# Turning the softmax tile p of a cross-attention kernel: from TensorE transposes to a transposing DMA of two float16 parts

## Chip, cores and metric

The kernel runs on one core of a Trainium2 chip. The metric is the device time of one execution in microseconds (us); lower is better. Engines: PE is TensorE (matmuls; PEld its weight loads), DVE is VectorE, ACT is ScalarE, POOL is GpSimd, SP is the sync engine, whose only work here is to issue DMAs.

## What is computed

One layer of cross-attention and one feed-forward product, in float32, for x of 32 batches x 64 tokens x 512 and a context of the same shape. All 32 query heads have width 128; 8 key/value heads are shared by four query heads each.

```python
q = rope(layernorm(x) @ Wq)        # 32 heads x 128
k = rope(ctx @ Wk); v = ctx @ Wv   # 8 heads x 128
s = q @ k.T / sqrt(128); s = where(mask == 0, -1e9, s)
p = softmax(s)                     # 64 x 64 per batch and head
x = x + (p @ v) @ Wo
x = x + layernorm(x) @ dequant(mxfp4(kernel)) + bias
```

## The kernel before, in words

**Precision by splitting.** Every operand of the large products is held as a high part (rounded to TensorE's fast 32-bit format, fp32r) and a low part (the rest). A product is then three matmuls (high x high, high x low, low x high), in the helper `three` (L539 to L541) and in `project_o` (L725 to L727). For p @ v two matmuls do: the 128 partitions of VS hold the high part of v in one half and the low part in the other; PS holds the high part of p in both halves, PL the low part of p in one half and zeros in the other (L703, L704).

**Stages and pairs.** The work is cut into 128 pairs m (PAIRS): one key/value head with its four query heads, for two batches of 64 tokens. A software pipeline runs over stages n; each engine has its own hand-written order within a stage, and all waits are semaphores. With m = n - 5, PE's stage n (L783 to L821) is `project_q(n)` (12 matmuls), `scores(m)` (4 products in 8 passes into pS), `turn_p(m-1)`, `values(m-2)`, then in some stages the K projection, the V projection, the FFN product, and `project_o(n-8)` (12 matmuls). The stages from n = 128 on have no `project_q`; in stages 130 to 136 there follow the last eight layer-norm and FFN tiles (`turn_f`, `ffn_high`, `ffn_low`).

**The path of p.** DVE masks the scores and takes the row maximum (L1336, L1339); ACT takes exp with the sum of each row (L1002); DVE takes the reciprocal and writes the normalised p to the SBUF tile sm (`p_scaled`, L1137 to L1145). One stage later PE turns sm in two 128x128 transposes into the PSUM tile pT (`turn_p`, L676 to L688). ACT casts two halves of pT to PS (`p_high`, L915), DVE subtracts to make PL (L1357 to L1361), ACT copies both halves of PS to the other partitions (L1007 to L1010), and one stage later PE uses them in `values` (L690 to L705).

**Orders around the change.** ACT's stage n is: `exchange` of the q tile for rope (L923, L924), rope tables, `v_high`, `x_high`, `f_high`, the weight casts `high` (L830), `p_high(m-1)`, exp(m), the PS copies, `out_high(m-2)` (L907), and `f_split_high`; from stage 130 on `out_high` stands ahead of exp. DVE's stage n begins with the sum of the output projection (`acc`, L1282), which waits for the end of PE's `project_o` of the stage before; then come layer-norm statistics, the low part of v, `f_low` (L1103) and `normalise` (L1067) in the last stages, rope's cos product, mask and maximum of pair m, the PL subtraction, steps of the mxfp4 quantisation (stages 10 to 55, in the other half of pT), `p_scaled(m)`, `out_low(m-2)`, and `ffn_add` (L1114). From stage 130 on `out_low` stands ahead of `p_scaled`.

**SP's queue.** SP runs one list of DMA issues, each behind its own wait (L492 to L529). In a stage n: the weight loads due in it, a raw x tile, stores, mask rows, and for the eight FFN tiles of the middle (f = 0 to 7, stages 69 to 76) the transposing DMA `turn_split(f)` (L470 to L478), which turns a 128 x 1024 float16 tile and which `ffn_high` waits for. From stage 130 on the store of FFN tile n-122 is issued in SP's stage n (L499, L500); it waits (L462) for the `ffn_add` of that tile, which DVE does in its stage n+1.

Of the kernel before, what the change touches and what calls it, by code (L numbers as in the profile page):

```python
# [86 lines left out]
PART = [range(0, 1), range(1, 4), range(4, 8)] + [range(k, k + 1) for k in range(8, QUANT)]  # L87

def quant_steps(n):  # L90

    parts = quant_parts(n)
    return sum(QUANT * i + PART[c].stop for i, c in parts[-1:]) if parts and parts[-1][1] < len(PART) else (
        QUANT * parts[-1][0] + QUANT if parts else 0)
# [29 lines left out]
def streamed(n):  # L124
    return [i for i, w in enumerate(STREAM) if w[0] == n]
# [48 lines left out]
def build(nc, x, ctxT, pos, mask, wq, wk, wv, wo, fkT, fbias, table, eye, out):  # L174
    ctx = ExitStack()
    with ctx:
        def sb(name, shape, dt):
            return ctx.enter_context(nc.sbuf_tensor(name, shape, dt))
# [8 lines left out]
        with ExitStack() as loads:  # L187
# [11 lines left out]
        kT = sb("kT", [128, 2, 512], F32)  # L199
        VS, PS = sb("VS", [128, 2, 8, 256], F32R), sb("PS", [128, 2, 256], F32R)  # L200
        QH, KH = sb("QH", [128, 4, 4, 128], F32R), sb("KH", [128, 4, 128], F32R)
# [4 lines left out]
        t2, t3 = sb("t2", [128, 512], F32), sb("t3", [128, 512], F32)  # L206
        PL = sb("PL", [128, 2, 256], F32R)
        sm = sb("sm", [128, 256], F32)
        ident = sb("ident", [128, 128], F32)
# [31 lines left out]

        d_ft = sem("d_ft")
# [3 lines left out]
        e_qk, e_pt, e_pv, e_op = sem("e_qk"), sem("e_pt"), sem("e_pv"), sem("e_op")  # L246
        e_ft, e_fm, e_wt = sem("e_ft"), sem("e_fm"), sem("e_wt")
# [3 lines left out]
        a_hi, a_xh, a_cs, a_ex = sem("a_hi"), sem("a_xh"), sem("a_cs"), sem("a_ex")  # L251
        a_ph, a_px, a_ah, a_vh, a_fh, a_w4 = (sem("a_ph"), sem("a_px"), sem("a_ah"), sem("a_vh"), sem("a_fh"),
                                              sem("a_w4"))
# [177 lines left out]
        def _(sp):  # L431
# [29 lines left out]
            def store(f):  # L461
# [73 lines left out]
        def _(pe):  # L535
# [49 lines left out]
            def ffn_high(f):  # L585
                b = bank(("m", f))
                if f < 8:
                    pe.wait_ge(d_ft, 16 * f + 16)
                else:
                    pe.wait_ge(a_fh, f + 1)  # L590
                if f == 15:
                    pe.wait_ge(v_pl, 2 * PAIRS)
# [82 lines left out]

            def turn_p(m):  # L676
                pe.wait_ge(v_pn, m + 1)
                if m:
                    pe.wait_ge(v_pl, 2 * m)
                else:  # L680
                    pe.wait_ge(*lo_made(PLACE["c", 1, 1]))
                steps = quant_steps(m + 5)
                if steps:
                    pe.wait_ge(v_q, steps)
                for hp in range(2):
                    made = pe.transpose(pT[:, 128 * hp:128 * hp + 128], sm[:, 128 * hp:128 * hp + 128],  # L686
                                        ident[:, :])
                made.then_inc(e_pt, 1)  # L688

            def values(m):  # L690
                s, p = m // 4, m % 4
                G = s // 2
                j = 4 * (s % 2) + p
                c = slice(128 * (G % 2), 128 * (G % 2) + 128)
                pe.wait_ge(v_pl, 2 * m + 2)
                if not m:
                    pe.wait_ge(v_const, 3)
# [85 lines left out]
            for n in range(OPENED, END):  # L783
# [41 lines left out]
        def _(act):  # L825
# [136 lines left out]
            for n in range(OPENED, END):  # L962
                m = n - 5

                if 0 <= n - 1 < PAIRS and n - 1 not in ALONE:
                    exchange(n - 1)
# [22 lines left out]

                if 0 <= m - 1 < PAIRS:  # L990
                    p_high(m - 1)
                if 0 <= m - 2 < PAIRS and n > PAIRS + 1:
# [12 lines left out]
                if PAIRS - 1 <= n <= PAIRS + 1:  # L1005
                    out_high(m - 2)
                if 0 <= m - 1 < PAIRS:  # L1007
                    for i in range(2):
                        act.wait_ge(a_ph, 2 * (m - 1) + i + 1)
                        act.copy(PS[ROWS[1 - i], i, :], PS[ROWS[i], i, :].bitcast(F32)).then_inc(a_px, 1)  # L1010
# [11 lines left out]
        def _(dve):  # L1022
# [114 lines left out]
            def p_scaled(m):  # L1137
                v4 = scores_place(m).rearrange("p (a k) -> p a k", a=4)
                dve.wait_ge(a_ex, m + 1)
                dve.reciprocal(rinv, rsum).then_inc(v_ri, 1)  # L1140
                dve.wait_ge(v_ri, m + 1)
                if m:
                    dve.wait_ge(e_pt, m)
                dve.tensor_tensor(sm.rearrange("p (a k) -> p a k", a=4), v4, rinv.unsqueeze(2).broadcast_to([128, 4, 64]),
                                  ALU.mult).then_inc(v_pn, 1)  # L1145

# [81 lines left out]

            for i in range(2):
                dve.memset(PL[ROWS[1 - i], i, :].bitcast(F32), 0.0).then_inc(v_const, 1)  # L1230
            statistics("x", 0)
# [41 lines left out]
            for n in range(OPENED, END):  # L1273
                m = n - 5
                if 0 <= n - 9 < PAIRS:
                    o = n - 9
                    j = o % 8
                    dve.wait_ge(e_op, o + 1)
                    if o % HALF < 8:
                        dve.wait_ge(d_x[j], 16 * (o // HALF) + 16)  # L1280
                    if o < PAIRS - 1:
                        dve.tensor_tensor(acc[:, j, :], pO[:, :], acc[:, j, :], ALU.add).then_inc(v_ac, 1)  # L1282
                    else:
                        last_sums()
                if n in X_AT and X_AT[n] >= 8:
                    statistics("x", X_AT[n])
# [68 lines left out]
                if n in FFN_AT and not is_last(n):  # L1355
                    normalise("f", FFN_AT[n])
                if 0 <= m - 1 < PAIRS:  # L1357
                    for i in range(2):
                        dve.wait_ge(a_ph, 2 * (m - 1) + i + 1)
                        dve.tensor_tensor(PL[ROWS[i], i, :], pT[ROWS[i], 0:256], PS[ROWS[i], i, :].bitcast(F32),  # L1360
                                          ALU.subtract).then_inc(v_pl, 1)  # L1361
                if 0 <= m - 2 < PAIRS and n > PAIRS + 1:
# [176 lines left out]
```

## Time and profile before

| What | Value |
|---|---|
| Time, median of 3 runs (lowest to highest) | 1138.07 us (1137.52 to 1138.55) |
| Span of the profiled execution, first to last instruction | 1136.2 us |
| PE busy in that span | 1126.4 us, 99% |
| DVE / ACT / POOL busy | 71% / 68% / 55% |
| DMA queue of SP, share of 16 engines | 18.3% |

The page gives no second time for the profiled execution; its span lies 1.9 us under the median of the timed runs, which also count what lies around the first and last instruction. A matmul's duration in the rows includes its pipeline latency, and consecutive matmuls overlap: what one costs on PE is the distance between starts, not its duration.

### The profile page before, as it was taken

Reading aid. Unit: us, or ns where it says so; the run is one execution under the profiler, and the core shown is the slowest. Engines: PE = TensorE matmul, PEld = TensorE weight load, DVE = VectorE, ACT = ScalarE, POOL = GpSimd, SP = SyncE. Lnnn points to the kernel's source line nnn. Section 1 sums busy time; section 2 is a strip of 40 time slices with the busy share of each in tenths; the row PEclk is TensorE's granted clock in tenths of the full one; section 3 lists DMA queues with packets and bytes.
Section 4 is the critical chain, followed back from the end, with each engine's and each line's share of the span. In section 5 each row is a group of like instructions: output and inputs, shape, how many; then the busy total and the mean of one; then the engine's idle time right before and its main releaser. Section 6 shows DMA issues by size and latency. Waiting matters only on the chain.

```text
span 1136.2 us, 19698 instructions
## 1 busy us (share of the span) xinstructions
PE 1126.4 (99%) x6315; PEld 971.5 (86%) x6326; DVE 810.1 (71%) x1753; ACT 769.0 (68%) x2306; POOL 629.6 (55%) x518
## 2 busy tenths in 40 slices
PE   7999999999999999999999999999999999999998
PEld 6888888888888888888888788888888888888886
DVE  7877777777777777688788756656566665656698
ACT  7866676566676766688766566676766677666763
POOL 7854645365554655569666556545654446545433
PEclk9999999999999999999999999999999999999999
DMA  8311211112111111224124421110201112020001
GB/s 260 86 34 43 75 39 46 33 43 66 35 51 33 61 39 37 93 71 142 48 68 111 116 75 43 38 48 20 83 10 29 48 38 65 11 73 20 1 7 69
DMA packets 60196, 65.57 MB, mean 58 GB/s; under 512 B 17216, under 2 KB 36032, under 8 KB 60096
## 3 DMA queue, kind: packets, MB, share of 16 engines
q1 hardware_dynamic: 59184, 61.96, 18.3%
q0 software_dynamic: 768, 2.10, 0.6%
q8 instruction: 53, 0.87, 0.3%
q14 instruction: 47, 0.39, 0.1%
q10 hardware_dynamic: 144, 0.26, 0.1%
HBM read 58.01 MB, written 4.19 MB: 55 GB/s over the span
## 4 chain that ended last, share of the span: by engine, by line
PE 98%; DMA 1%; DVE 0%; POOL 0%; issue 0%; DVEq 0%
PE proj L539 15%; PE proj L540 15%; PE proj L541 15%; PE pS L671 9%; PE pO L725 9%; PE pO L726 9%; PE pO L727 9%; PE pV L703 3%; PE pV L704 3%; PE pO L735 3%; PE pT L686 3%; PE pO L738 1%; PE proj L602 1%; PE proj L595 1%; PE proj L553 1%; DMA t<-table,tiny 1%
## 5 line engine op out<-in xcount | busy, mean ns | idle before, releaser
L915 ACT CAST PS<-pT 64x256 fp32r<-64x256 f32 x256 | 93.8, 367 | 296.9 <-PE pV L704 293.5
L1436 POOL TENSOR_TENSOR t<-t,SIN 128x512 f32<-128x512 f32 x124 | 159.7, 1288 | 185.9 <-ACT t L924 185.5
L539 PE MATMUL proj<-XH,QH 128*128 128x512 f32 x500 | 195.7, 391 | 0.0
L541 PE MATMUL proj<-XH,QL 128*128 128x512 f32 x500 | 194.8, 390 | 0.0
L540 PE MATMUL proj<-XL,QH 128*128 128x512 f32 x500 | 194.7, 389 | 0.0
L725 PE MATMUL pO<-OH,AH 128*128 128x512 f32 x432 | 171.6, 397 | 0.0
L726 PE MATMUL pO<-OL,AH 128*128 128x512 f32 x432 | 169.2, 392 | 0.0
L727 PE MATMUL pO<-OH,AL 128*128 128x512 f32 x432 | 168.5, 390 | 0.0
L1440 POOL TENSOR_TENSOR qT<-qT,t 128x512 f32<-128x512 f32 x124 | 159.8, 1289 | 9.7
L1156 DVE TENSOR_TENSOR qT<-proj,COS 128x512 f32<-128x512 f32 x128 | 88.4, 690 | 95.1 <-PE proj L541 55.5
L1002 ACT ACTIVATE pS<-pS,tiny 128x64 f32<-128x64 f32 x504 | 140.7, 279 | 7.7 <-DVE tiny L1339 3.6
L671 PEld LDWEIGHTS pS<-kT,qT 128*128 128x128 f32 x1008 | 131.8, 191 | 10.0 <-issue 0.2
L1446 POOL TENSOR_TENSOR kT<-kT,t 128x512 f32<-128x512 f32 x31 | 40.1, 1295 | 168.5 <-DVE t L1131 168.5
L1149 DVE TENSOR_TENSOR AL<-pV,AH 128x512 fp32r<-128x512 f32 x128 | 88.4, 691 | 62.4 <-ACT AH L907 62.0
L671 PE MATMUL pS<-kT,qT 128*128 128x64 f32 x1008 | 125.8, 268 | 0.0
L1360 DVE TENSOR_TENSOR PL<-pT,PS 64x256 fp32r<-64x256 f32 x256 | 107.5, 420 | 24.8 <-ACT PS L915 20.7
L1404 POOL TENSOR_TENSOR OL<-OR,OH 128x512 fp32r<-128x512 f32 x62 | 79.8, 1296 | 61.2 <-ACT OH L830 61.1
L541 PEld LDWEIGHTS proj<-XH,QL 128*128 128x128 f32 x500 | 93.9, 188 | 19.6
L539 PEld LDWEIGHTS proj<-XH,QH 128*128 128x128 f32 x500 | 93.9, 188 | 19.1
L540 PEld LDWEIGHTS proj<-XL,QH 128*128 128x128 f32 x500 | 93.9, 188 | 19.1
L1010 ACT CAST PS<-PS 64x256 fp32r<-64x256 f32 x256 | 103.5, 404 | 6.2
L1002 ACT ACTIVATION_READ_ACCUMULATOR pS<-pS,tiny 128x1 f32 x504 | 100.5, 199 | 1.5
(216 smaller groups left out, 2581.4 us busy)
## 6 DMA issues: line engine op xcount, KB each, us to landing
QR<-wq SPq DMA_DIRECT2D x64, 256.0 KB, 2.6
OR<-wo SPq DMA_DIRECT2D x62, 256.0 KB, 3.2
CR<-ctxT SPq DMA_DIRECT2D x16, 256.0 KB, 5.1
KR<-wk SPq DMA_DIRECT2D x16, 256.0 KB, 2.6
UR<-wv SPq DMA_DIRECT2D x16, 256.0 KB, 3.9
acc<-x SPq DMA_DIRECT2D x15, 256.0 KB, 3.8
out<-acc SPq DMA_DIRECT2D x15, 256.0 KB, 2.3
rawx<-x SPq DMA_DIRECT2D x8, 256.0 KB, 2.9
```

The lines of the kernel that those rows point to most:

```text
L539: pe.matmul(dst, lh, rh, start=k == 0, stop=False)
L540: pe.matmul(dst, lh, rl, start=False, stop=False)
L541: made = pe.matmul(dst, ll, rh, start=False, stop=k == last)
L671: made = pe.matmul(v[:, 128 * hp + 64 * b:128 * hp + 64 * b + 64], qT[:, s % 2, 2 * p + b, 2 * hp:2 * hp + 2, :].rearrange("p h t -> p (h ...
L725: pe.matmul(pO[:, :], AH[:, m % 2, h], oh, start=h == 0, stop=False)
L726: pe.matmul(pO[:, :], AH[:, m % 2, h], ol, start=False, stop=False)
L727: made = pe.matmul(pO[:, :], AL[:, m % 2, h], oh, start=False, stop=h == 3)
L1002: made = act.activation(v4[:, a], v4[:, a], ACT.Exp, bias=nmx[:, a:a + 1], accum_out=rsum[:, a:a + 1])
L1010: act.copy(PS[ROWS[1 - i], i, :], PS[ROWS[i], i, :].bitcast(F32)).then_inc(a_px, 1)
L1360: dve.tensor_tensor(PL[ROWS[i], i, :], pT[ROWS[i], 0:256], PS[ROWS[i], i, :].bitcast(F32), ALU.subtract).then_inc(v_pl, 1)
L1436: pool.tensor_tensor(t[:, :], t[:, :], SIN[:, 512 * (s % 2):512 * (s % 2) + 512], ALU.mult).then_inc(g_qs, 1)
L1440: pool.tensor_tensor(dst, dst, t[:, :].rearrange("p (a t) -> p a t", t=64), ALU.add).then_inc(g_qr, 1)
```

## The change

p is turned by a DMA, not by PE. `p_scaled` now multiplies by 2^14 as well and writes into PSUM (sm is now half of pT). ACT's `p_high` rounds it to float16, each 64-wide block twice; DVE's `p_low` writes the rest, as float16, between zeros that are set once.
```diff
@@ SP, the list of stages, then its helpers @@
             for n in range(FIRST, END):
                 if n:
                     load_stream(streamed(n))
+                if 0 <= n - 6 < PAIRS:
+                    turn_p(n - 6)
...
+            def turn_p(m):
+                if m:
+                    sp.wait_ge(a_ps, m)
+                sp.wait_ge(a_ph, m + 1)
+                sp.wait_ge(v_pl, m + 1)
+                sp.dma_start(PT16[:, :, :], P16[:, :], transpose=True).then_inc(d_pt, 16)
...
@@ PE @@
-                if 0 <= m - 1 < PAIRS:
-                    turn_p(m - 1)
...
-                pe.wait_ge(v_pl, 2 * m + 2)
-                pe.wait_ge(a_px, 2 * m + 2)
+                pe.wait_ge(a_ps, m + 1)
...
                 for b in range(2):
-                    pe.matmul(pV[:, b], VS[:, b, j, c], PS[:, b, :], start=True, stop=False)
-                    made = pe.matmul(pV[:, b], VS[:, b, j, c], PL[:, b, :], start=False, stop=True)
+                    dst = pV[:, b].rearrange("p (h t) -> p h t", h=2)
+                    pe.matmul(dst, VS[:, b, j, c], PS[:, b:4:2], start=True, stop=False)
+                    made = pe.matmul(dst, VS[:, b, j, c], PS[:, 4 + b::2], start=False, stop=True)
...
@@ ACT @@
             def p_high(m):
-                act.wait_ge(e_pt, m + 1)
-                if m:
-                    act.wait_ge(e_pv, m)
-                for i in range(2):
-                    act.copy(PS[ROWS[i], i, :], pT[ROWS[i], 0:256]).then_inc(a_ph, 1)
+                act.wait_ge(v_pn, m + 1)
+                if m:
+                    act.wait_ge(d_pt, 16 * m)
+                act.activation(P16[:, 0:512].rearrange("p (a d k) -> p a d k", a=4, d=2),
+                               sm.rearrange("p (a k) -> p a k", a=4).unsqueeze(2).broadcast_to([128, 4, 2, 64]),
+                               ACT.Copy).then_inc(a_ph, 1)
+
+            def p_turned(m):
+                act.wait_ge(d_pt, 16 * m + 16)
+                if m:
+                    act.wait_ge(e_pv, m)
+                act.activation(PS[:, :, :], PT16[:, :, :], ACT.Copy, scale=1.0 / P_SCALE).then_inc(a_ps, 1)
...
@@ DVE @@
+            def p_low(m):
+                dve.wait_ge(a_ph, m + 1)
+                v = sm.rearrange("p (h i k) -> p h i k", h=2, i=2)
+                high = P16[:, 0:512].rearrange("p (h i d k) -> p h i d k", h=2, i=2, d=2)[:, :, :, 0, :]
+                dve.tensor_tensor(P16[:, 512:1024].rearrange("p (h u k) -> p h u k", h=2, u=4)[:, :, 0:4:3, :],
+                                  v, high, ALU.subtract).then_inc(v_pl, 1)
...
-    nc = _bacc.Bacc("TRN2", target_bir_lowering=False, num_devices=1)
+    nc = _bacc.Bacc("TRN2", target_bir_lowering=False, num_devices=1, dynamic_dma_scratch_size=4096)
```

## Rows read from the trace of the kernel before

**Rows 1.** The page: the span and what each engine was busy.

```profile
span 1136.2 us, 19698 instructions
PE 1126.4 (99%) x6315; PEld 971.5 (86%) x6326; DVE 810.1 (71%) x1753; ACT 769.0 (68%) x2306; POOL 629.6 (55%) x518
```

**Rows 2.** The page's chain that ended last, share of the span by engine.

```profile
PE 98%; DMA 1%; DVE 0%; POOL 0%; issue 0%; DVEq 0%
```

**Rows 3.** Timeline of PE, stage 5 (no p to turn yet): start, us, instruction.

```profile
35.86 1.00 PE L671 MATMUL pS<-kT,qT 128*128 128x64 f32 x8
...
36.88 0.28 PE L540 MATMUL proj<-UL,CH 128*128 128x256 f32 x1
```

**Rows 4.** Timeline of PE, stage 79, up to the second matmul behind the transposes.

```profile
676.23 1.00 PE L671 MATMUL pS<-kT,qT 128*128 128x64 f32 x8
...
677.41 0.28 PE L704 MATMUL pV<-PL,VS 128*128 128x256 f32 x1
```

**Rows 5.** Groups of instructions: count | busy us, mean ns | idle before, releaser.

```profile
L686 PE MATMUL pT<-ident,sm 128*128 128x128 f32 x256 | 49.8, 276 | 0.0
L915 ACT CAST PS<-pT 64x256 fp32r<-64x256 f32 x256 | 93.8, 367 | 296.9 <-PE pV L704 293.5
L1010 ACT CAST PS<-PS 64x256 fp32r<-64x256 f32 x256 | 103.5, 404 | 6.2
L1360 DVE TENSOR_TENSOR PL<-pT,PS 64x256 fp32r<-64x256 f32 x256 | 107.5, 420 | 24.8 <-ACT PS L915 20.7
L830 ACT CAST QH<-QR 128x512 fp32r<-128x512 f32 x64 | 39.7, 621 | 10.1 <-DMA QR<-wq 9.0
L858 ACT ACTIVATE qT<-acc,tiny 128x512 f32<-128x512 f32 x6 | 4.9, 818 | 4.9 <-DVE tiny L1073 4.9
```

**Rows 6.** The eight transposing DMAs of line 478: from issue to landing.

```profile
DMA to landing us min/median/max: 3.1/3.1/4.6
```

**Rows 7.** Timeline of DVE and PE, rest of stage 79 and start of 80.

```profile
680.44 0.42 DVE L1144 TENSOR_TENSOR sm<-pS,tiny 128x256 f32<-128x256 f32 x1
...
680.51 0.39 PE L539 MATMUL proj<-XH,QH 128*128 128x512 f32 x1
...
683.24 1.00 PE L671 MATMUL pS<-kT,qT 128*128 128x64 f32 x8
```

**Rows 8.** Timeline of SP, DVE and PE around stage 75, FFN tile 6.

```profile
638.53 1.25 SPq L478 DMA_TRANSPOSE F<-rawx  x1
...
639.44 0.69 DVE L1282 TENSOR_TENSOR acc<-pO,acc 128x512 f32<-128x512 f32 x1 [0.40 <-PE pO L727]
...
643.50 1.04 PE L595 MATMUL proj<-W,F 128*128 128x512 bf16 x4
```

**Rows 9.** Timeline of DVE, SP and PE, stages 131 to 134.

```profile
1105.80 0.68 DVE L1114 TENSOR_TENSOR acc<-proj,acc 128x512 f32<-128x512 f32 x1
...
1106.51 0.34 SPq L468 DMA_DIRECT2D out<-acc  x1
...
1107.83 0.36 PE L703 MATMUL pV<-PS,VS 128*128 128x256 f32 x1
...
1108.13 0.68 DVE L1103 TENSOR_TENSOR F<-proj,F 128x512 f16<-128x512 f32 x1
...
1112.18 0.68 DVE L1114 TENSOR_TENSOR acc<-proj,acc 128x512 f32<-128x512 f32 x1
...
1113.46 0.36 PE L703 MATMUL pV<-PS,VS 128*128 128x256 f32 x1
...
1114.51 0.68 DVE L1103 TENSOR_TENSOR QR<-proj,QR 128x512 f16<-128x512 f32 x1
...
1117.23 0.68 DVE L1114 TENSOR_TENSOR acc<-proj,acc 128x512 f32<-128x512 f32 x1
...
1118.75 0.47 PE L703 MATMUL pV<-PS,VS 128*128 128x256 f32 x1
```

**Rows 10.** Groups: PE's first matmuls, behind 4.9 us without work.

```profile
L744 PE MATMUL pT<-ident 128*128 128x128 f32 x10 | 2.8, 427 | 4.9 <-DMA ident<-eye 4.9
```

More of the change, by code:

```diff
@@ L30 @@
 MASKED = -3.0e38
+P_SCALE = 2.0 ** 14
 FIRST = 0
@@ L87 @@
 PART = [range(0, 1), range(1, 4), range(4, 8)] + [range(k, k + 1) for k in range(8, QUANT)]
[L90 to L94, printed above, removed]
 def quant_parts(n):
@@ L199, in build @@
         kT = sb("kT", [128, 2, 512], F32)
-        VS, PS = sb("VS", [128, 2, 8, 256], F32R), sb("PS", [128, 2, 256], F32R)
+        VS, PS = sb("VS", [128, 2, 8, 256], F32R), sb("PS", [128, 8, 128], F32R)
         QH, KH = sb("QH", [128, 4, 4, 128], F32R), sb("KH", [128, 4, 128], F32R)
@@ L206, in build @@
         t2, t3 = sb("t2", [128, 512], F32), sb("t3", [128, 512], F32)
-        PL = sb("PL", [128, 2, 256], F32R)
-        sm = sb("sm", [128, 256], F32)
+        P16, PT16 = sb("P16", [128, 1024], FP16), sb("PT16", [128, 8, 128], FP16)
         ident = sb("ident", [128, 128], F32)
@@ L229, in build @@
         pT = pb("pT", [128, 512])
+        sm = pT[:, 0:256]
         pV = pb("pV", [128, 2, 256])
@@ L240, in build @@
         d_rawx, d_rawm = [sem("d_rawx0"), sem("d_rawx1")], sem("d_rawm")
-        d_ft = sem("d_ft")
+        d_ft, d_pt = sem("d_ft"), sem("d_pt")
         d_cs = [sem(f"d_cs{j}") for j in range(8)]
         e_xt, e_ct, e_qp, e_kp, e_vp = sem("e_xt"), sem("e_ct"), sem("e_qp"), sem("e_kp"), sem("e_vp")
-        e_qk, e_pt, e_pv, e_op = sem("e_qk"), sem("e_pt"), sem("e_pv"), sem("e_op")
+        e_qk, e_pv, e_op = sem("e_qk"), sem("e_pv"), sem("e_op")
         e_ft, e_fm, e_wt = sem("e_ft"), sem("e_fm"), sem("e_wt")
@@ L251, in build @@
         a_hi, a_xh, a_cs, a_ex = sem("a_hi"), sem("a_xh"), sem("a_cs"), sem("a_ex")
-        a_ph, a_px, a_ah, a_vh, a_fh, a_w4 = (sem("a_ph"), sem("a_px"), sem("a_ah"), sem("a_vh"), sem("a_fh"),
+        a_ph, a_ps, a_ah, a_vh, a_fh, a_w4 = (sem("a_ph"), sem("a_ps"), sem("a_ah"), sem("a_vh"), sem("a_fh"),
                                               sem("a_w4"))
@@ L591, in ffn_high @@
                 if f == 15:
-                    pe.wait_ge(v_pl, 2 * PAIRS)
+                    pe.wait_ge(v_pl, PAIRS)
                 for c, dst in ffn_halves(f):
@@ L674, in scores @@
                 made.then_inc(e_qk, 1)
-            def turn_p(m):
-                pe.wait_ge(v_pn, m + 1)
-                if m:
[L679 to L688, printed above, removed]
             def values(m):
@@ L694, in values @@
                 c = slice(128 * (G % 2), 128 * (G % 2) + 128)
-                pe.wait_ge(v_pl, 2 * m + 2)
-                if not m:
-                    pe.wait_ge(v_const, 3)
-                pe.wait_ge(a_px, 2 * m + 2)
+                pe.wait_ge(a_ps, m + 1)
                 pe.wait_ge(v_vl, v_count(s - 2 * (G % 2), p))
@@ L963, in _ @@
                 m = n - 5
+                if 0 <= m - 2 < PAIRS:
+                    p_turned(m - 2)
                 if 0 <= n - 1 < PAIRS and n - 1 not in ALONE:
@@ L988, in _ @@
                     x_normalise(15)
-                if 0 <= m - 1 < PAIRS:
-                    p_high(m - 1)
                 if 0 <= m - 2 < PAIRS and n > PAIRS + 1:
@@ L1006, in _ @@
                     out_high(m - 2)
[L1007 to L1010, printed above, removed]
                 if 0 <= m - 2 < PAIRS and n < PAIRS - 1:
                     out_high(m - 2)
+                if 0 <= m < PAIRS:
+                    p_high(m)
                 if n in FFN_AT and not is_last(n):
@@ L1142, in p_scaled @@
                 if m:
-                    dve.wait_ge(e_pt, m)
-                dve.tensor_tensor(sm.rearrange("p (a k) -> p a k", a=4), v4, rinv.unsqueeze(2).broadcast_to([128, 4, 64]),
-                                  ALU.mult).then_inc(v_pn, 1)
+                    dve.wait_ge(a_ph, m)
+                else:
+                    dve.wait_ge(a_cs, 8)
+                    dve.wait_ge(a_xh, 8)
+                dve.scalar_tensor_tensor(sm.rearrange("p (a k) -> p a k", a=4), v4, P_SCALE,
+                                         rinv.unsqueeze(2).broadcast_to([128, 4, 64]), ALU.mult,
+                                         ALU.mult).then_inc(v_pn, 1)
+            def p_low(m):
[4 more added lines that the diff above has]
+                                  v, high, ALU.subtract).then_inc(v_pl, 1)
             def out_low(m):
@@ L1227, in _ @@
             dve.memset(mhalf, -0.5).then_inc(v_const, 1)
-            for i in range(2):
-                dve.memset(PL[ROWS[1 - i], i, :].bitcast(F32), 0.0).then_inc(v_const, 1)
+            dve.memset(P16[:, 512:1024].bitcast(F32), 0.0).then_inc(v_const, 1)
             statistics("x", 0)
@@ L1284, in _ @@
                         last_sums()
+                if 0 <= m - 1 < PAIRS:
+                    p_low(m - 1)
                 if n in X_AT and X_AT[n] >= 8:
@@ L1356, in _ @@
                     normalise("f", FFN_AT[n])
[L1357 to L1361, printed above, removed]
                 if 0 <= m - 2 < PAIRS and n > PAIRS + 1:
```

## The prediction

> **What bounds the kernel.** I read the page first: PE is busy for 1126.4 of the 1136.2 us of the span, and no other engine reaches three quarters [rows 1]. The chain that ended last is PE for 98% [rows 2]. So I take PE as the bound from start to end, and ask two things of every edit: what it takes off PE's own list, and whether its result still reaches PE in time. Busy shares cannot answer the first, because matmuls overlap; I go by distances between starts in PE's timeline.
>
> The two transposes of a pair are 256 matmuls of 276 ns, 49.8 us of busy time [rows 5]. They do not cost that. Stage 5 runs scores with nothing to turn: from the start of the scores to the second matmul of what follows it is 36.88 - 35.86 = 1.02 us [rows 3]. In stage 79, with two transposes between, the same distance is 677.41 - 676.23 = 1.18 us [rows 4]. I measure to the second matmul since the first behind the 4-byte passes is slow in both. The transposes cost 0.16 us of PE per pair.
>
> **The sum, part by part.**
>
> *PE's list.* 128 pairs x 0.16 = 20.5 us less. The ends of the cost are 0 (if the switch from scores to values costs more than stage 5 shows) and 49.8 us (the busy time); I take the two timelines, which are the same work with and without. `values` still makes four matmuls of 256 columns, so nothing is added. The wait for the quantisation steps ends nothing now: PE's chain has no such piece.
>
> *ACT.* Removed: 2 x 367 + 2 x 404 = 1.54 us per pair [rows 5]. Added: `p_high`, 512 wide, at least 0.62 like the 128x512 casts of L830, and `p_turned`, 1024 wide. From 256 to 512 elements the casts go from 404 to 621 ns, so 1024 is 0.62 + 2 x 0.217 = 1.05 us. The other end is the ACTIVATE of L858, 818 ns for 512: 0.82 and 1.64 us. So ACT goes from 1.54 to 1.67 (taken, a copy with a constant scale is nearest to the casts) or 2.46 us. ACT is busy 68% of the span [rows 1] and waits 293.5 us for PE's `values` alone [rows 5]; that wait covers it and is itself removed.
>
> *DVE.* Two subtractions of 420 ns become one of about that [rows 5]; `p_scaled` keeps its shape. 0.42 us less per pair, worth nothing while PE is the bound.
>
> *The new path, in a plain stage.* A plain stage lasts 683.24 - 676.23 = 7.01 us [rows 4, 7], 6.85 after the change; S is the start of its scores. `sm` is ready at S + 4.63 [rows 7], `p_high` at S + 5.3. PE's output projection ends at S + 4.3, where `project_q` begins [rows 7]. DVE's `acc` (0.69) [rows 8] may be pushed back a little by `out_low`; with `p_low` (0.42) the tile is ready near S + 6. The transposing DMA lands 3.1 us after issue [rows 6]: S + 9.1. `p_turned` stands behind the next `p_high`, at S + 6.85 + 5.3 = S + 12.1, so ACT does not wait for the DMA, and is done at S + 13.2; `values` needs it at S + 13.7 + 0.8 = S + 14.5. In this stage the landing may be 3 us later before ACT waits, 4 before PE does. Cost taken: 0. SP's weight loads stand ahead of `turn_p` and those of the next stage wait for a later PE event anyway; loads gain at most the 1.25 us of one transposing issue [rows 8], and they are made stages ahead of their use. SP's queue fills 18.3% of the 16 DMA engines (the table); 128 transfers more leave room.
>
> *FFN tiles of the middle.* `turn_split` now stands behind `turn_p` in SP's queue, and `turn_p` waits for DVE's `acc` and `p_low`. For tile 6 that is 639.44 + 0.69 + 0.42 + 0.1 = 640.65, plus 1.25 us of issue = 641.9, plus 3.1 = 645.0, where it was issued at 638.53 before; PE wants it at 643.50 - 0.16 = 643.3 [rows 6, 8]. A stall of 1.6 us, and the same in the stage after. The other six have V (twelve matmuls) or K as well between scores and FFN, and come out about even. 3.4 us in all; the ends are 0 and, if each landed in 4.6 us, 3.4 + 8 x 1.5 = 15.
>
> *The last stages.* Without `project_q` a stage is 4.3 us (676.23 to 680.51) [rows 4, 7]. The path from scores to cast needs about 5.3 + 0.42 + 3.1 + 1.05 = 9.9 us plus semaphores, and PE gives it 2 x 4.3 + 0.8 = 9.4. I take 1.7 us of stalls over stages 129 and 130.
>
> Then SP's queue turns round. The store of FFN tile 8 is in SP's stage 130 and waits for an `ffn_add` of DVE's stage 131; `turn_p(125)` is queued behind it. That `ffn_add` ends at 1105.80 + 0.68, the store takes 0.34 from 1106.51, so the turn is issued at 1106.9, lands at 1110.0, is cast by 1111.1; PE wants it at 1107.83 - 0.17 = 1107.67 [rows 9]. Stall 3.4 us.
> From this cast the next is a closed ring: `f_high` 0.6 (behind `p_turned` on ACT), from `f_low` to the end of `ffn_add` 1112.86 - 1108.13 = 4.7, the store 0.5, the turn 3.1, the cast 1.05: 10.0 us. PE's own work between is 1113.46 - 1107.83 - 0.17 = 5.5 [rows 9]. Stall 4.6 us (0.1 from rounding and gaps).
> The third ring has no scores: 1117.91 - 1114.51 = 3.4, less the two PL subtractions (0.84) = 2.6, so 0.6 + 2.6 + 0.5 + 3.1 + 1.05 = 7.9 against 1118.75 - 1113.46 = 5.3 [rows 9]. Stall 2.6 us.
> Tail: 1.7 + 3.4 + 4.6 + 2.6 = 12.3 us. Ends: 8 (half the small ones, and a faster path to the store) and 19 (landing 4.6, casts at the ACTIVATE price in all three rings).
>
> *Start.* ACT is full in stages 5 to 8; up to 0.7 us, taken as 0.7.
>
> *Sum.* Against the profiled span: 1136.2 - 20.5 + 3.4 + 12.3 + 0.7 = 1132.1. The timed median lies 1.9 above the span: 1134.0 us, 0.36% less than 1138.07. About 0.2% (2.3 us) can be told from no change.
>
> **A price from the notes.** Rows 6 price a turn of eight 128x128 blocks at 3.1 us from issue to landing. The Trainium skill, VectorE: DVE Perf Modes, section "The three transpose paths", puts one 128x128 block by DMA at 1309 ns against 390 for TensorE, and its rules choose TensorE where PSUM will do. By 8 x 1.309 = 10.5 us a turn would come over 3 us too late for PE in every plain stage, some 1138 + 120 x 3 = 1500 us. The eight turns of the trace contradict it, so this rival gets less than 0.01, counted in D.
>
> **The rivals.**
>
> *A, as summed: 1134.0, chance 0.50.* Own range 1129 to 1140.
>
> *B, the tail mostly hides, 0.10.* If the small stalls vanish and the rings run with the shortest pieces (tail 8, middle 0), or PE saves 0.2 us per pair (25.6), the time is 1124 to 1129. Against it: the store's wait is in program order, so the first 3.4 us are nearly certain.
>
> *C, the clock after the stalls, 0.17.* PE would stand still for over 3 us twice near the end. Its first ten 128x128 transposes, behind 4.9 us without work, took 427 ns each where later ones take 276 [rows 5, 10]. If PE drops to its lower clock after the long stalls, the rings hide most of it, but `values` and the matmuls behind the last stall do not: about 3 us, 1137.0, no change by the bound. Against: those first matmuls stand at a cold start, and the stalls have work between them. The Trainium skill, TensorE: Matmul & The Clock Gate, section "What's actually happening", gives 1.2 GHz after idleness and 2.4 GHz when warm; by it this case would be the likely one.
>
> *D, ACT becomes the bound (slower), 0.15.* Place: the 7.01 us stages, some 50 of them. ACT has now `p_high` waiting for `sm`, then `p_turned`, `exchange` and up to two weight casts before the next exp. With casts at 818 ns per 512 it gains 2.46 - 1.54 = 0.92 us per pair. It decides from the point where ACT's list exceeds 6.85 us. At 0.3 us over, for 50 stages, it costs 15 us: 1149. For it: `p_turned` is an ACTIVATE with a scale, like L858. Against: L858 reads a bias and a scale per partition, this one constants.
>
> *E, the start or the DMA queues, 0.06.* GpSimd's gathers get a smaller descriptor scratch, or weight loads come late behind turns: 2 to 6 us on A, 1138.
>
> *F, the transposes cost PE nothing, 0.02.* PE's switch from scores to values costs what they did: 1134 + 20.5 = 1154.5. Stage 5 speaks against it.
>
> **How the numbers follow.** A's own range falls to three quarters below 1135.8. Faster: 0.75 x 0.50 + 0.10 + 0.03 (C) = 0.50. Slower: D and F 0.17, half of E 0.03, A's upper edge 0.03 = 0.23. Same: the rest, 0.27. The range reaches from B's middle to the milder half of D: 1127 to 1144.
>
> **What would show it.** In the profile after: no PE row of `turn_p`; distance from scores to the second `values` matmul 1.02 us in all pairs; plain stages of 6.85 us without PE waits; 128 more transposing DMAs landing in 3.1 us; `p_turned` near 1.05 us. PE idle before `values` for ACT's `p_turned` near 3.4, 4.6 and 2.6 us in the last three pairs, before the FFN of tiles 6 and 7 near 1.6 us. I am wrong if PE waits appear in the plain stages, if `p_turned` takes 1.6 us, or if the store of tile 8 does not hold `turn_p(125)`.

## The result, and the profile after

The changed kernel takes **1141.44 us** (median of 9 runs, 1139.42 to 1142.62) against 1138.07 for the kernel before in the same session (9 runs, 1137.52 to 1138.94). The ratio is 1.0028, 95% interval 1.0019 to 1.0037: slower by 0.3%, where 0.4% faster was forecast. The time is inside the range, the direction is wrong. The profiled execution, from which the stretches below are read, is the slowest of these nine (1142.62 us), so they add up to 4.3 us and not to the 3.4 us between the medians.

The page after, span and busy time of each engine, answers to [rows 1]:

```profile
span 1140.5 us, 18940 instructions
PE 1114.0 (98%) x6070; PEld 954.6 (84%) x6070; DVE 738.3 (65%) x1624; ACT 757.2 (66%) x2050; POOL 630.0 (55%) x518
```

Its chain that ended last, by engine, answers to [rows 2]:

```profile
PE 82%; DVE 5%; issue 4%; ACT 3%; DMA 3%; POOL 1%; SPq 1%; ACTq 0%; DVEq 0%; POOLq 0%
```

PE is busy for 12.4 us less and the span is 4.3 us longer. The chain was PE for 98%; now it leaves PE for DVE, ACT and DMA. So PE was relieved, and then made to wait. Where it waits is the view of waits after, engine PE (total us, times, longest); before, its three rows were the start alone (4.9, 0.9 and 0.3 us), and two such rows are left out here:

```profile
PE pV L691 <- ACT PS L908: 10.0, 7, 4.1
PE proj L599 <- DMA F<-rawx: 5.9, 7, 1.6
...
PE proj L543 <- ACT t L917: 1.1, 2, 0.8
PE pS L675 <- DVE pT L1138: 0.8, 1, 0.8
```

First what was gained. PE's timeline after, stage 131 (pair 126), where PE has no transposes, answers to [rows 4]:

```profile
1092.19 1.00 PE L675 MATMUL pS<-kT,qT 128*128 128x64 f32 x8
1093.00 0.36 PE L691 MATMUL pV<-PS,VS 128*128 128x256 f32 x1
1093.20 0.28 PE L692 MATMUL pV<-PS,VS 128*128 128x256 f32 x1
```

From scores to the second `values` matmul it is 1.01 us, where it was 1.18. It is 1.01 in 121 stages after and 1.18 in 122 before. The stages without waits are shorter by just that: 7.01 became 6.84, 8.45 became 8.27, 11.19 became 11.02. Over 127 distances between scores this is 21.6 us. Against that line of -0.17 us a stage, the starts of the scores show where it was given back:

| stretch | given back, us | PE's waits in it, us |
|---|---|---|
| stages 6 to 8 (start) | 3.4 | 0.84 for `p_scaled`, 0.41 for `p_turned` |
| stages 59 to 67 (tiles of x) | 1.7 | 0.29 and 0.77 for the exchange copy of L917 |
| stages 68 to 76 (FFN tiles) | 7.0 | seven for the FFN's turned tile, 5.9 in all |
| stages 127 to 131 | 1.2 | 0.54, 0.40, 0.45 for `p_turned` |
| all other stages | 0.2 | none |
| from the last scores to the end | 12.6 (42.01 for 29.39) | 4.09, 2.19, 1.90 for `p_turned` |

With 0.2 us saved ahead of the first scores: -0.2 - 21.6 + 3.4 + 1.7 + 7.0 + 1.2 + 0.2 + 12.6 = +4.3 us, the difference of the spans.

The new instructions stand in the groups after (count | busy us, mean ns | idle before, releaser), answering to [rows 5]:

```profile
L908 ACT ACTIVATE PS<-PT 128x1024 fp32r<-128x1024 f16 x128 | 134.8, 1053 | 5.1 <-DMA PT<-P 5.1
L900 ACT ACTIVATE P<-pT 128x512 f16<-128x512 f32 x128 | 76.5, 597 | 53.0 <-DVE pT L1138 40.6 <-DMA PT<-P 12.4
```

`p_turned` takes 1053 ns and `p_high` 597, so 1.65 us a pair on ACT for 1.54 before. Over the span ACT did not fill: its busy time fell from 769.0 to 757.2 us (68 to 66%). The rows of the two new casts overlap, as those below show: `p_turned` starts 0.50 us after `p_high`, whose row lasts 0.60.

The new path in a plain stage, in the timeline after; it answers to [rows 7]:

```profile
663.14 0.60 ACT L900 ACTIVATE P<-pT 128x512 f16<-128x512 f32 x1 [0.23 <-DVE pT L1138]
663.64 1.05 ACT L908 ACTIVATE PS<-PT 128x1024 fp32r<-128x1024 f16 x1
...
667.33 1.23 SPq L470 DMA_TRANSPOSE PT<-P  x1
...
668.74 1.00 PE L675 MATMUL pS<-kT,qT 128*128 128x64 f32 x8
```

The turn is issued 1.4 us ahead of the next scores, and ACT casts the tile of the pair before right behind its `p_high`, without a wait: nothing here touches PE.

**The tail.** SP, DVE, ACT and PE of the last stages after, in the timeline; it answers to [rows 9]:

```profile
1096.45 0.68 DVE L1105 TENSOR_TENSOR acc<-proj,acc 128x512 f32<-128x512 f32 x1
...
1097.16 0.35 SPq L462 DMA_DIRECT2D out<-acc  x1
1097.61 2.40 SPq L470 DMA_TRANSPOSE PT<-P  x1
...
1101.95 0.60 ACT L900 ACTIVATE P<-pT 128x512 f16<-128x512 f32 x1 [6.08 <-DMA PT<-P]
1102.44 1.05 ACT L908 ACTIVATE PS<-PT 128x1024 fp32r<-128x1024 f16 x1
...
1103.54 0.58 PE L691 MATMUL pV<-PS,VS 128*128 128x256 f32 x1 [4.09 <-ACT PS L908]
...
1107.93 0.68 DVE L1105 TENSOR_TENSOR acc<-proj,acc 128x512 f32<-128x512 f32 x1
...
1108.64 0.35 SPq L462 DMA_DIRECT2D out<-acc  x1
1109.09 1.28 SPq L470 DMA_TRANSPOSE PT<-P  x1
...
1112.28 0.60 ACT L900 ACTIVATE P<-pT 128x512 f16<-128x512 f32 x1 [4.94 <-DMA PT<-P]
...
1113.88 0.39 PE L691 MATMUL pV<-PS,VS 128*128 128x256 f32 x1 [2.19 <-ACT PS L908]
...
1121.44 0.38 PE L691 MATMUL pV<-PS,VS 128*128 128x256 f32 x1 [1.90 <-ACT PS L908]
```

It is the forecast ring: DVE's `ffn_add`, SP's store, the turn behind it, ACT's cast, PE. Measured from the last scores, the three `values` start 4.1, 8.8 and 11.1 us later than before (5.09, 15.43, 22.99 us against 0.98, 6.61, 11.90), so the rings add 4.1, 4.7 and 2.3 us; 3.4, 4.6 and 2.6 were forecast. The rest of the 12.6 us, 1.5, comes behind the last stall: from there to the end it is 19.02 us for 17.49. The windows of that stretch (window, length, busy us of PE, PEld, DVE, ACT and POOL, granted clock, DMA share, GB/s) say why:

```profile
1104.00:1106.00 2.00, 2.00 (x8) 1.71 (x8) 1.97 (x6) 0.59 (x1) 1.25 (x2) 0.50 0.00 0
...
1110.00:1114.00 4.00, 1.81 (x9) 0.71 (x8) 1.31 (x4) 1.72 (x3) 0.00 (x0) 1.00 0.41 86
...
1124.00:1126.00 2.00, 2.00 (x6) 1.54 (x5) 0.24 (x1) 0.00 (x0) 0.41 (x1) 0.50 0.37 133
```

The granted clock is 0.50, the lower level of 1.2 GHz, after the first and the third stall, and 1.00 around the second. In the middle it costs nothing, because the ring is longer than PE's own work (PE then waits 2.19 us in place of the 4.6 forecast); at the end it is paid in full.

**The FFN tiles.** The same view around stage 75, answering to [rows 8]:

```profile
635.90 0.69 DVE L1283 TENSOR_TENSOR acc<-pO,acc 128x512 f32<-128x512 f32 x1 [1.17 <-PE pO L715]
...
636.51 0.41 DVE L1146 TENSOR_TENSOR P<-pT,P 128x256 f16<-128x256 f32 x1
...
637.01 1.23 SPq L470 DMA_TRANSPOSE PT<-P  x1
638.35 1.27 SPq L480 DMA_TRANSPOSE F<-rawx  x1
...
638.42 1.00 PE L675 MATMUL pS<-kT,qT 128*128 128x64 f32 x8
...
641.56 1.08 DVE L1058 TENSOR_SCALAR rawx<-acc,tiny 128x512 f32<-128x512 f32 x1 [1.22 <-DMA F<-rawx]
641.60 1.02 PE L599 MATMUL proj<-W,F 128*128 128x512 bf16 x4 [1.65 <-DMA F<-rawx]
```

`turn_p` waits for DVE's `acc` and `p_low`; `turn_split` stands behind it. PE waits 1.65 us here and 1.63 in the next stage, as forecast (1.6 each). But five of the other six tiles made PE wait too, 2.6 us in all (0.59 in stage 69, then 1.04, 0.29 and 0.20, and 0.47 in stage 74). These rows after, of stages 69 to 71, show how:

```profile
571.28 2.48 SPq L480 DMA_TRANSPOSE F<-rawx  x1
...
575.68 0.55 DVE L1058 TENSOR_SCALAR rawx<-acc,tiny 128x512 f32<-128x512 f32 x1 [3.46 <-DMA F<-rawx]
...
581.29 0.69 DVE L1283 TENSOR_TENSOR acc<-pO,acc 128x512 f32<-128x512 f32 x1
...
602.12 0.69 DVE L1283 TENSOR_TENSOR acc<-pO,acc 128x512 f32<-128x512 f32 x1 [0.65 <-PE pO L715]
```

The first tile's `turn_split` took SP 2.48 us to issue. Where it took 1.25 or 2.11 (the traces of e5 and e1, whose edits leave these stages alone) PE has no wait in stage 69, where it took 2.46 (e9) it waits 0.80. The landing also ends a wait of DVE: `normalise` of the next tile waits for it, 11.9 us in seven tiles. In stage 69 DVE stood idle for it for 3.46 us and then had 0.3 us of idle time before `acc`, which came 11.88 us behind the scores for 10.47 before; the next turns were issued late by that, and PE waited 1.04 us. Stage 73, with 2.96 us of idle DVE, and the 0.47 us of stage 74 look the same. That is a ring through DVE which the forecast did not have. In stages 70 to 72, 74 and 75 DVE had caught up: its `acc` waits for PE's output projection there (0.65 us in the row of stage 71). So the waits of 0.29 and 0.20 us are the queue's order alone, in stages that the forecast called even.

### The profile page after: what moved, and what is told of

It reads as the page before. It is cut to its first block, busy times and chain, and to the rows that moved or that the text cites. A ratio compares the mean times of both kernels' runs of the same rounds, so it can differ in the third digit from the quotient of the medians.

```text
span 1140.5 us, 18940 instructions
## 1 busy us (share of the span) xinstructions
PE 1114.0 (98%) x6070; PEld 954.6 (84%) x6070; DVE 738.3 (65%) x1624; ACT 757.2 (66%) x2050; POOL 630.0 (55%) x518
## 4 chain that ended last, share of the span: by engine, by line
PE 82%; DVE 5%; issue 4%; ACT 3%; DMA 3%; POOL 1%; SPq 1%; ACTq 0%; DVEq 0%; POOLq 0%
PE proj L543 13%; PE proj L545 13%; PE proj L544 13%; PE pO L713 8%; PE pO L714 8%; PE pO L715 8%; PE pS L675 8%; PE pV L691 3%; DMA F<-rawx 2%; PE pO L723 2%; PE pV L692 2%; PE pO L726 1%; SPq L470 1%; PE proj L599 1%; ACT PS L908 1%
## 5 line engine op out<-in xcount | busy, mean ns | idle before, releaser
L995 ACT ACTIVATE pS<-pS,tiny 128x64 f32<-128x64 f32 x504 | 143.6, 285 | 280.7 <-DVE tiny L1342 280.7
L675 PEld LDWEIGHTS pS<-kT,qT 128*128 128x128 f32 x1008 | 131.7, 191 | 11.1 <-issue 1.2
L908 ACT ACTIVATE PS<-PT 128x1024 fp32r<-128x1024 f16 x128 | 134.8, 1053 | 5.1 <-DMA PT<-P 5.1
L1283 DVE TENSOR_TENSOR acc<-pO,acc 128x512 f32<-128x512 f32 x127 | 87.3, 688 | 73.5 <-PE pO L715 69.1
L900 ACT ACTIVATE P<-pT 128x512 f16<-128x512 f32 x128 | 76.5, 597 | 53.0 <-DVE pT L1138 40.6
L715 PEld LDWEIGHTS pO<-OH,AL 128*128 128x128 f32 x432 | 81.5, 189 | 17.8
```

What stands on the lines that cost most here:

```text
L675: made = pe.matmul(v[:, 128 * hp + 64 * b:128 * hp + 64 * b + 64], qT[:, s % 2, 2 * p + b, 2 * hp:2 * hp + 2, :].rearrange("p h t -> p (h ...
L715: made = pe.matmul(pO[:, :], AL[:, m % 2, h], oh, start=False, stop=h == 3)
L908: act.activation(PS[:, :, :], PT16[:, :, :], ACT.Copy, scale=1.0 / P_SCALE).then_inc(a_ps, 1)
L995: made = act.activation(v4[:, a], v4[:, a], ACT.Exp, bias=nmx[:, a:a + 1], accum_out=rsum[:, a:a + 1])
```

## The theory, and what stood against it

Theory Q: the time was lost in the order of SP's queue, in two places, and nowhere by the DMA itself: the stores of the last FFN tiles ahead of `turn_p` (tail), and `turn_p` ahead of `turn_split` (FFN). Rivals: the 128 transposing DMAs are slow or crowd the others; ACT's order (`p_turned` ahead of the exchange) makes a ring at the start; PE's clock does it. Times below are medians, ratios are to the kernel before.

## Experiments: the order of SP's queue

**e1.** Changed kernel, the stores of tiles 8 to 15 one stage later, as those of tiles 0 to 7 already are:

```diff
-                if n - 1 > PAIRS and n - 1 in FFN_AT:
-                    store(FFN_AT[n - 1])
...
-                if n - 2 in FFN_AT and n - 2 < PAIRS:
+                if n - 2 in FFN_AT:
                     store(FFN_AT[n - 2])
```

> Edit: the stores of FFN tiles 8 to 15 move one stage later in SP's list, so that turn_p of pairs 125 to 127 is no longer queued behind a store that waits for the next stage's ffn_add. Theory Q (queue order): PE's three waits before values (4.1, 2.2 and 1.9 us in the changed kernel) shrink to under 1 us each, the granted clock stays at 1.00 to the end, and the last part (from the last scores to the end, 42.1 us) falls to 30 to 31 us: 1141.4 - 11.5 = 1130 us. Rival D (the transposing DMAs themselves are slow or crowd the engines): turn_p lands as late as now, 1138 to 1141 us.

Measured: 1130.08 us, ratio 0.9929 (0.9912 to 0.9945). The same view of PE's waits as above, of this kernel:

```profile
PE proj L597 <- DMA F<-rawx: 5.2, 6, 1.7
...
PE pV L689 <- ACT PS L906: 1.8, 4, 0.5
```

The three long waits are gone, those of the FFN stay. 11.4 us of the time lay in where a store of 0.35 us stands. That the time is a hit to the tenth is in part luck: by the two profiles the last part alone is 13.0 us shorter (29.04 us for 42.01), and in this execution the granted clock was 0.50 once in the FFN stretch (640 to 643 us, behind a stall of 1.62), which gave back 7.8 us for 7.0.

**e2.** Changed kernel, `turn_split` ahead of `turn_p`:

```diff
+                if n - 1 in FFN_AT and n - 1 < PAIRS:
+                    turn_split(FFN_AT[n - 1])
                 if 0 <= n - 6 < PAIRS:
                     turn_p(n - 6)
...
-                if n - 1 in FFN_AT and n - 1 < PAIRS:
-                    turn_split(FFN_AT[n - 1])
```

> Edit: in SP's list turn_split of the middle FFN tiles stands ahead of turn_p of the same stage, not behind it. Theory Q: turn_split is issued about 3 us earlier, PE's waits before the FFN matmuls (5.9 us in seven stages) go, and stages 69 to 76, now 7.0 us longer than 0.17 us per stage would give, lose 6 us of that: 1135.5 us. turn_p comes 1.3 us later and costs nothing. Rival D: two transposing DMAs in one stage are what costs, whichever is first: 1139.5 to 1141.5 us.

Measured: 1132.72 us, ratio 0.9957 (0.994 to 0.9973), 8.7 us less than the changed kernel. No wait for the FFN's tile is left in the view of waits, and the FFN stretch gives back 0.0 us for 7.0: with the order on SP the ring through DVE is gone too. The gain was more than expected: its three tail waits were 3.69, 3.10 and 0.34 us for 4.09, 2.19 and 1.90, and its last part is 2.0 us shorter. In its profile the start also gave back 1.7 us and not 3.4, which is the clock (below), not this edit.

## Experiments: the order of ScalarE's casts

**e3.** Changed kernel, `p_turned` moved behind exchange, rope and `v_high`:

```diff
-                if 0 <= m - 2 < PAIRS:
-                    p_turned(m - 2)
                 if 0 <= n - 1 < PAIRS and n - 1 not in ALONE:
                     exchange(n - 1)
...
                     v_high(n - 1)
+                if 0 <= m - 2 < PAIRS:
+                    p_turned(m - 2)
```

> Edit: ACT's p_turned moves from the head of its stage to behind exchange, the rope tables and v_high. Theory R (a ring of ACT and DVE limits the short stages at the start: exp, p_scaled, p_high, p_turned, exchange, v_high, low part of v, cos, mask, exp, 7.97 us a round): the round shortens by 1.05 us, stages 7 and 8 lose about 2 of their 3.4 us, and stages 61 to 65 (PE waits there for exchange) lose 1.3 of 1.8 us: 1138 us. Rival S (ACT is simply overfull at the start): no change there, since ACT's work is the same: 1141 us.

Measured: 1142.86 us, ratio 1.0043 (1.0027 to 1.006): a miss. PE's waits:

```profile
PE pV L691 <- ACT PS L908: 13.0, 14, 3.1
```

The waits for the exchange copy and `p_scaled` went; 1.28 and 1.26 us for `p_turned` stand at the start in their place, 0.92 in an x stage and 0.32 once in a cycle of 16 pairs, five times, which had none. The start gave back 3.0 us, at a granted clock of 1.00; with the cast in its first place it is 1.7 to 1.8 at that clock (below), so the move costs 1.2 us there.

**e4**, all three moves together:

> All three reorderings together. Theories Q and R: the gains add, 1141.4 - 11.5 - 6 - 3.3 = 1120.6 us, some 1.5% under the kernel before, and what is left over the ideal (1136.2 - 21.8 + 1.9 = 1116.3 us) is 4 us of short-stage stalls. Rival D: 1137 us or more.

Measured: 1124.87 us, ratio 0.9884 (0.9867 to 0.99). Faster than both kernels, and 4 us short of the sum, since e3's part costs: its trace has the same start waits (1.22 and 1.26 us) and the same five of 0.3 us.

**e7**, the two moves on SP alone:

> The changed kernel with both moves on the sync queue (stores of tiles 8 to 15 a stage later, the FFN's transposing DMA ahead of p's) and with the cast of p left where the change put it. If the three losses (tail, FFN stages, start) stand apart and add up: the two moves gave 11.4 and 8.7 us alone, of which the tail part of the second (about 1.5 us: its waits were 3.69, 3.10 and 0.34 in place of 4.09, 2.19 and 1.90 at a higher clock) is inside the first, so 1141.4 - 11.4 - 7.2 = about 1122.5 us, and less than the kernel with all three moves by 2 to 3 us, since putting the cast later cost 1.4 alone. No wait of TensorE over 0.1 us between stage 68 and 76 and none over 0.6 after stage 127. If instead the late cast had helped inside the three, this run stands above 1124.9.

Measured: **1121.64 us** (1121.48 to 1122.95), ratio 0.9859 (0.9843 to 0.9876): the best version of the study, 16.4 us under the kernel before. Its page and PE's waits:

```profile
span 1119.5 us, 18940 instructions
PE 1106.7 (99%) x6070; PEld 949.7 (85%) x6070; DVE 740.9 (66%) x1624; ACT 756.4 (68%) x2050; POOL 631.2 (56%) x518
```

```profile
PE pV L689 <- ACT PS L906: 1.8, 4, 0.5
...
PE proj L541 <- ACT t L915: 1.0, 2, 0.7
```

The losses add up: -21.6 + 1.8 (start) + 1.7 (x) + 0.0 (FFN) + 1.2 + 0.6 (others) - 0.3 (tail) = -16.6, beside -16.7 between the two spans and -16.4 between the medians. The same 128 transposing DMAs run here, so the rival that they are slow or crowd the queues is refuted as a cause of the lost time.

**e8.** e7 with `p_turned` right behind the exchange, ahead of rope and `v_high`:

```diff
-                if 0 <= m - 2 < PAIRS:
-                    p_turned(m - 2)
                 if 0 <= n - 1 < PAIRS and n - 1 not in ALONE:
                     exchange(n - 1)
+                if 0 <= m - 2 < PAIRS:
+                    p_turned(m - 2)
```

> The kernel with both moves on the sync queue, and ScalarE casts the turned p right behind the two exchange copies instead of ahead of them (1.17 us later, not the 2 us and more of the run that put it behind v_high too). If the x stages' two waits of TensorE (0.28 and 0.75 us, for the second exchange copy) come of the cast's 1.05 us ahead of the copies, they go, the values' products find their operand ready in plain stages, and the time falls by 1 to 2 us from 1121.6: 1119.7 to 1120.7. If it is ScalarE's work altogether in these stages and not its order, a wait of the same size stands elsewhere (for the cast, before the values' products) and the time stays at 1121.6; more than 1123 if plain stages wait for the cast too, as 0.32 us once in a cycle of 16 pairs did where it came last.

Measured: 1126.67 us, ratio 0.9895 (0.9879 to 0.9912): a miss, 5.0 us slower than e7. In the x stages a wait of 0.57 us for `p_turned` replaced the two for the exchange, and the stretch gave back 1.65 us as before (1.70). At the start PE waited 0.44 and 1.74 us for the cast, and then:

```profile
58.00:61.00 3.00, 2.87 (x13) 2.87 (x14) 2.16 (x5) 2.36 (x6) 1.55 (x2) 0.50 0.48 93
61.00:64.00 3.00, 3.00 (x11) 2.52 (x10) 1.61 (x5) 2.57 (x11) 2.92 (x3) 0.50 0.20 60
```

Six microseconds at half the clock; the start gave back 5.9 us for 1.8. The other stages gave back 3.0 us for 0.6: five of them have a wait of 0.30 us for the cast, as in e3, where e7 has none. By the spans that is nearly all of the difference (6.3 us; the profiled execution is the slowest of four). The clock is not all of it: this kernel's fastest execution had a granted clock of 1.00 over its span and took 1125.31 us, 3.7 more than e7's median. So twice a later cast did not remove the x stages' loss (1.8 and 1.65 us for 1.7) and made the start worse; the cast's first place was the best of the three. That the remaining loss comes of the length of the path through ACT and DVE is argued, not shown: no run shortened that path. It stays open, for some 3.5 us.

## Experiments: TensorE's gain and its clock

**e6.** Changed kernel with two transposes of the identity into pV between scores and `values` of every pair:

```diff
+                if m:
+                    pe.wait_ge(v_al, m)
+                for hp in range(2):
+                    pe.transpose(pV[:, hp, 0:128], ident[:, :], ident[:, :])
                 pe.wait_ge(a_ps, m + 1)
                 pe.wait_ge(v_vl, v_count(s - 2 * (G % 2), p))
-                if m:
-                    pe.wait_ge(v_al, m)
```

> The changed kernel with two 128x128 transposes of the identity put back between each pair's scores and values, into pV, as many and as large as the two that the change took out; nothing waits for them. It undoes TensorE's gain alone. If a stage was 0.17 us shorter because of these two, undisturbed stages grow back to their old length (7.01 for 6.84, 8.45 for 8.27) and the time is up to 128 x 0.17 = 21.8 us longer, less what the stalls hide (about 5): 1158 to 1163. If the shorter stages came of something else (fewer waits, the products' other order of columns), the time stays within 3 us of 1141.4.

Measured: 1156.78 us, ratio 1.0168 (1.0151 to 1.0185), 15.3 us more than the changed kernel and a little under the range expected. The undisturbed stages are back at 7.01, 8.45 and 11.19 us, and so is the distance from scores to the second `values` matmul (1.18 us):

```profile
690.92 1.00 PE L675 MATMUL pS<-kT,qT 128*128 128x64 f32 x8
691.76 0.39 PE L688 MATMUL pV<-ident 128*128 128x128 f32 x2
...
692.10 0.28 PE L694 MATMUL pV<-PS,VS 128*128 128x256 f32 x1
```

So two such transposes cost the 0.17 us a stage that the change had gained. The stalls hid more than the 5 us allowed: the last part is 3 us shorter than in the changed kernel, the FFN's waits are 4.9 us for 5.9, and the start gave back 1.8 us, not 3.4.

**e5.** Changed kernel; PE is kept busy in its last three stalls by transposes whose result the next product overwrites:

```diff
+                if m >= PAIRS - 3:
+                    pe.wait_ge(v_al, m)
+                    for _ in range({125: 32, 126: 36, 127: 16}[m]):
+                        pe.transpose(pV[:, 0, 0:128], ident[:, :], ident[:, :])
                 pe.wait_ge(a_ps, m + 1)
```

> The changed kernel, and at the end TensorE is kept busy in its three stalls by 32, 36 and 16 transposes of the identity into a place that the next product overwrites, before the values' products of pairs 125, 126 and 127. The waits on the rings of p stay as long as they are (they are not TensorE's). If the granted clock of 0.50 in the last 40 us comes of the stalls before it and costs what the last stretch is longer than before (19.06 against 17.49 us from pair 127's values to the end), the clock is granted 1.00 to the end and the time is 1.6 us less and up to 2 more where the weight of the clock also lay on the ring: 1138.5 to 1140. If the clock falls for another reason, it falls here too and the time stays at 1141.4 or grows.

Measured: 1141.32 us, ratio 1.0031 (1.002 to 1.0043), no different from the changed kernel: a miss. Its trace says why: 0.44 us of the first stall was left, and 1.00 was granted behind it; 2.10 us of the second was left, and 0.50 was granted for some 3 us:

```profile
1100.00:1105.00 5.00, 4.56 (x27) 3.68 (x26) 4.05 (x10) 3.35 (x12) 1.84 (x2) 1.00 0.00 2
...
1113.00:1116.00 3.00, 3.00 (x10) 2.50 (x10) 2.65 (x5) 0.73 (x2) 1.83 (x2) 0.50 0.01 3
```

The second ring was also 1.3 us longer than in the changed kernel, because its transposing DMA took SP 2.44 us to issue where that one took 1.28.

**e9**, the same with 36, 50 and 18 transposes:

> As the run that kept TensorE busy at the end, with 36, 50 and 18 transposes for 32, 36 and 16. There the filled stall (0.44 us left) was followed by a granted clock of 1.00 and the one of 2.10 us left by 0.50 for 3 us. If the clock follows the stall, no stretch of the last 40 us is granted less than 1.00 here, and from pair 125's values to the end no matmul of 512 columns is 0.43 us from the next; the last part (from pair 127's scores) is then 38.5 us where the ring is 10.3 and 7.6 us long, 40 where a transposing DMA's issue takes 2.4 us in place of 1.3 once more. If the clock has another cause, 0.50 shows again somewhere in 1100 to 1130.

Measured: 1140.61 us, ratio 1.0022 (1.0012 to 1.0032). Its windows grant 1.00 from 1095 to 1135, for instance

```profile
1108.00:1112.00 4.00, 4.00 (x39) 4.00 (x38) 0.01 (x1) 0.64 (x2) 0.00 (x0) 1.00 0.52 131
1112.00:1116.00 4.00, 4.00 (x28) 3.60 (x27) 3.76 (x8) 1.97 (x3) 1.83 (x2) 1.00 0.01 2
```

and the last part is 1.4 us shorter than in the changed kernel (38.8 for 40.2, from the last scores to the issue of the last store). Behind the start of the last `values` it is 17.4 us to the end, as in the kernel before (17.49), for 19.02 in the changed one. So in these traces the clock follows PE's stalls and costs the tail about 1.4 us. The medians differ by 0.8 us with overlapping intervals, so the timed runs alone would not show it.

**The start.** The changed kernel's own profile and those of e1, e2, e5, e7 and e9, which leave the first 60 us untouched, have the same waits there (0.84 and 0.41 us). Yet it gave back 3.4 us in the one and 1.7 to 1.8 in the others. The windows of the changed kernel, then of e1:

```profile
58.00:61.00 3.00, 3.00 (x13) 2.71 (x12) 2.24 (x5) 2.29 (x5) 1.63 (x2) 0.50 0.64 135
```

```profile
58.00:61.00 3.00, 3.00 (x20) 2.63 (x18) 2.04 (x5) 2.46 (x6) 1.43 (x2) 1.00 0.61 125
```

The clock fell behind the same stalls in one execution and not in others; 1.6 us of this profile's start are that. Such a loss is not peculiar to this execution: over the span the granted clock is 0.994 in seven of the changed kernel's nine timed executions, the profiled one among them, 0.993 in one and 0.997 in the fastest (1139.42 us). Where it fell in those without a trace is not known; in e1 it was the FFN stretch.

## Why the prediction was wrong

- **The bound and PE's gain: right.** 0.16 us a pair from two timelines, not the 276 ns of a busy row; measured 0.17, and put back by e6.
- **ACT: right.** 1.05 us for `p_turned` (1053 ns measured), 0.62 for `p_high` (597 ns). Rival D (casts at 818 ns for 512) did not happen.
- **The plain stage at cost 0: right.** The other stages gave back 0.2 us in all, and PE has no wait in them.
- **The tail: mechanism right, sizes near, in part by luck.** 1.7 + 3.4 + 4.6 + 2.6 was forecast; 1.4 + 4.1 + 4.7 + 2.3 was measured, and e1 took the three long waits away by the store's place alone. The 1.7 had no working and was put on two stages; three share the 1.4. In the first ring three errors partly cancel: the turn was issued 0.9 us earlier against the last scores than I had it (0.84 ahead of them for 0.05 behind), it landed 4.3 us after issue and not 3.1, its issue taking 2.40 us of SP where 1.25 was assumed, and between the landing and the cast stands ACT's `p_high`, 0.5 us that I left out of the first two rings.
- **FFN tiles of the middle: the step that failed first.** "The other six have V (twelve matmuls) or K as well between scores and FFN, and come out about even": they did not. 7.0 us was given back for 3.4; e2, which only puts `turn_split` ahead of `turn_p`, takes all of it away. The two tiles that were priced came out right (1.65 and 1.63 us). In the others I asked who on PE waits for the landing and missed DVE's `normalise`, which twice handed the lateness to the next tile (1.04 and 0.47 us); the sum of two more was short by 0.2 to 0.3 us, and one slow issue cost 0.59. The split among these is read from the traces; no run separates them.
- **The x tiles: a term that was missing.** I gave the start up to 0.7 us because ACT is full there, and looked at no other stretch where it is; 1.7 us.
- **Start: mis-sized.** 0.7 forecast, 1.8 measured, 3.4 where the clock fell.
- **Rival C was wrongly made an alternative.** It came on top of A: 1.4 to 1.6 us at the tail, 1.6 at the start of this execution. I had worked out the stalls of A and then summed A at full clock. The traces have 0.50 behind the stalls of 4.09 and 1.90 us, and 1.00 behind the one of 2.19 us between them. The Trainium skill, TensorE: Matmul & The Clock Gate, section "What's actually happening", gives 1.2 GHz after idleness; the first and the third stall agree with it, the second does not.
- **The rival by price of a block: rightly given nothing.** From issue to the wait's end at ACT the eight blocks of a turn took 1112.28 - 1109.09 = 3.2 us. The Trainium skill, VectorE: DVE Perf Modes, section "The three transpose paths", gives 1309 ns for one block; the trace contradicts it as a price to multiply by eight.

Against the spans: the forecast 1132.1 becomes 1132.1 - 1.1 (PE) + 3.6 (FFN) + 2.7 (start) + 1.7 (x) + 1.5 (tail: 13.8 for 12.3) = 1140.5, as measured. No single miss turned the sign: the forecast was 4.1 us under the span before and the result is 4.3 over it. The largest are 3.6 us in the other FFN tiles and some 3 from the clock, in the start and the tail.

## What to carry to other kernels

A transfer moved past others in an in-order queue is priced by what it waits for, for everything behind it: here two lines moved in SP's queue turned a loss of 3.4 us into a gain of 16.4. When a result will land later, list every engine that waits for that landing, not only the bound one, and ask whether the lateness comes back to its own cause. When a forecast contains stalls of PE, its clock belongs to that same sum.

## What was not expected of the hardware

- **Two transposes in the dense stream cost PE 0.17 us, 0.08 each**, though a row shows 276 ns for one; 32 of them in a row (e5) took 3.66 us, 0.11 each.
- **The clock after a stall is not a matter of its length alone.** Behind 4.09 and 1.90 us it was 0.50, behind 2.19 between them 1.00; behind 0.84 and 0.41 at the start 0.50 in the changed kernel's profile and 1.00 in others with the same instructions.
- **The issue of one transposing DMA holds SP 1.23 us as a rule, but over 1.4, and up to 2.7, for one to four of the 136 in each run with the change**: the first turn at 41 us in seven of ten runs, the first FFN tile's (2.48 in the changed kernel), and one in the tail (2.40 in the changed kernel, 2.44 in e5, 1.78 in e7). In the tail it lies in the ring. What makes it longer was not tried.
